# Four projections of a graph kernel: rows and weights of the next layer requested inside the layer in front of it, four count groups per row tile beside the last layer, the first prefix product moved

## The reference

```python
x1 = relu(x @ W_ah + b_ah)
for W, a_src, a_dst, b in three layers:
    h = (x1 @ W).reshape(N, 4, 192)
    as_n = (h * a_src).sum(-1)
    ad_n = (h * a_dst).sum(-1)
    # then attention over the edges
```

## Time and profile before

| | us |
|---|---|
| median of three runs | 3877.01 |
| lowest and highest | 3874.04, 3880.10 |
| the profiled execution | 3876.07 |
| its span in the profile | 3874.40 |

### The profile page before, as it was taken

The page is one execution under the profiler, slowest core; times in us unless marked ns, Lnnn a source line. Parts: engine busy times, 40 slices in busy tenths (PEclk is TensorE's granted clock), DMA queues, the critical chain, the costliest instruction groups (busy, mean ns, idle before and its releaser), DMA issues.

```text
span 3874.4 us, 59093 instructions
## 1 busy us (share of the span) xinstructions
PE 3519.8 (91%) x19026; PEld 2968.0 (77%) x19027; DVE 1948.6 (50%) x2699; ACT 1684.3 (43%) x2913; POOL 2210.9 (57%) x1621
## 2 busy tenths in 40 slices
PE   6998967999979899578888999999999999999898
PEld 3555536999979899422233599999999999999898
DVE  8244788888633545697875532332323232331034
ACT  1112687888843321277878133333333333333221
POOL 7887873666620000139991177777777777776400
PEclk9999997999999999788989999999999999999999
DMA  5343202323242311322111576767676766765421
GB/s 189 74 115 98 59 4 53 94 77 92 56 139 77 122 37 68 114 68 58 44 52 49 175 190 167 181 157 182 155 182 160 179 169 168 180 157 110 94 84 64
DMA packets 175521, 435.21 MB, mean 112 GB/s; under 512 B 39950, under 2 KB 62501, under 8 KB 175398
## 3 DMA queue, kind: packets, MB, share of 16 engines
q0 software_dynamic: 69184, 193.10, 23.3%
q1 hardware_dynamic: 91878, 214.54, 17.2%
q10 hardware_dynamic: 14336, 26.07, 1.9%
HBM read 301.01 MB, written 132.24 MB: 112 GB/s over the span
## 4 chain that ended last, share of the span: by engine, by line
PE 50%; POOL 7%; issue 3%; ACT 3%; DVE 2%; DMA 1%; SPq 0%; ACTq 0%; POOLq 0%; DVEq 0%
PE ps L2090 30%; PE ps L2077 7%; POOL xplain L1410 6%; PE ps L1684 5%; PE ps L302 4%; PE ps L310 2%; ACT work L1312 1%; ACT ps L1303 1%; POOL drec L1395 1%; PE ps L328 0%; PE ps L1249 0%; PE ps L1816 0%; DMA ct<-x_d 0%; DMA xplain<-gat_d 0%; DMA drec<-keyrow_d 0%
## 5 line engine op out<-in xcount | busy, mean ns | idle before, releaser
L2090 PE MATMUL ps<-wsplit,xsplit 128*128 x6840 | 1233.9, 337 | 0.0
L2090 PEld LDWEIGHTS ps<-wsplit,xsplit 128*128 128x128 f32 x6840 | 1179.2, 188 | 0.0
L2130 ACT ACTIVATE ct<-ps,invs 128x768 f32<-128x768 f32 x190 | 171.1, 900 | 916.5 <-PE ps L2090 916.5
L1982 DVE CAST wsplit<-wplain 128x768 fp32r<-128x768 f32 x210 | 124.6, 593 | 854.2 <-PE ps L2090 836.4
L1312 ACT ACTIVATE work<-ps,work 128x418 f32<-128x418 f32 x720 | 433.7, 620 | 158.4 <-PE ps L1220 152.7
L1259 PE MATMUL ps<-hbuf,work 128*128 128x193 f32 x2400 | 455.2, 327 | 15.6 <-DVE work L1174 13.1
L2021 POOL TENSOR_TENSOR xsplit<-ct,xsplit 128x768 fp32r<-128x768 f32 x190 | 449.0, 2363 | 0.2
L1259 PEld LDWEIGHTS ps<-hbuf,work 128*128 128x128 f32 x2400 | 407.3, 190 | 43.5 <-issue 16.9
L1160 DVE SCALAR_TENSOR_TENSOR work<-work,cnt 128x1250 f32<-128x1250 f32 x240 | 352.4, 1468 | 160.4 <-ACT work L1312 159.3
L1303 ACT ACTIVATE ps<-work,lr 128x418 f32<-128x418 f32 x720 | 426.7, 624 | 6.4 <-DMA work<-lrow_d 6.4
L2016 POOL DMA_INDIRECT ct<-x_d,relrec x190 | 205.7, 1082 | 325.7 <-PE ps L2077 321.8
(11 more groups left out here) (234 smaller groups left out, 4571.0 us busy)
## 6 DMA issues: line engine op xcount, KB each, us to landing
wplain<-in_L_gnn_W_rel SPq DMA_DIRECT2D x34, 2304.0 KB, 12.3
work<-lrow_d SPq DMA_DIRECT2D x47, 625.0 KB, 3.8
feat_d<-work ACTq DMA_DIRECT2D x30, 386.0 KB, 3.8
hbuf<-feat_d SPq DMA_DIRECT2D x60, 193.0 KB, 2.5
gat_d<-work POOLq DMA_DIRECT2D x12, 960.0 KB, 5.2
xplain<-gat_d SPq DMA_DIRECT2D x30, 384.0 KB, 3.2
work<-xa_d SPq DMA_DIRECT2D x27, 384.0 KB, 3.3
wplain<-x_d SPq DMA_DIRECT2D x20, 384.0 KB, 3.0
```

Source lines behind the costliest of these rows:

```text
L2090: last = pe.matmul(ps[:, 4 + 2 * (u % 2) + h, 0:HALF], x[:, u, c * P:(c + 1) * P], w7[:, bass.ds(base + (lo * KC * D + c * D + h * HALF), ...
```

## The change

The diff, cut where only lines move or comments differ:

```diff
+            def open_rows(self, pe):
                 pe.wait_ge(self.turned, self.b["turned"] + 0)
+                pe.sem_inc(self.turned, 2 * self.K)
+
+            def open(self, pe, rows_opened=False):
+                if not rows_opened:
+                    self.open_rows(pe)
                 pe.wait_ge(self.product, self.b["product"])
-                pe.sem_inc(self.turned, 2 * self.K)
                 pe.sem_inc(self.product, 2)
...
                     turn(0, 0, 0)
                     others_out()
                     turn(0, 1, 0)
+                    weights()
                     with pe.Fori(0, NT // 2 - 1) as i:
                         for u in range(2):
                             times(i, u)
                             turn(i + 1, u, 0)
+                    if behind is not None:
+                        behind.open_rows(pe)
                     for u in range(2):
                         times(NT // 2 - 1, u)
...
                 def times(j):
                     pe.wait_ge(self.emptied, self.b["emptied"] + j + 2)
                     for h in range(2):
+                        if h:
+                            between(j, 2)
...
                 for j in range(NT):
                     pe.wait_ge(self.taken, self.b["taken"] + j + 1)
+                    between(j, 0)
                     if j + 1 < NT:
                         turn(j + 1)
-                    between(j, 0)
+                    if j == NT - 2 and behind is not None:
+                        behind.open_rows(pe)
+                    between(j, 1)
                     times(j)
-                    between(j, 1)
+                    between(j, 3)
...
-            for u in range(2):
-                sp.wait_ge(s_x1[u], 16 * (NT // 2 + 1))
             for l in range(3):
-                if l:
-                    sp.wait_ge(W_AH.product, (W_AH if l == 1 else W_H[0]).all_products)
-                    W_H[l].load(sp)
-                sp.wait_ge(W_AH.turned, (W_AH if l == 0 else W_H[l - 1]).all_turned)
-                W_H[l].stream(sp)
+                for j in range(NT):
+                    if l == 0:
+                        sp.wait_ge(s_x1[j % 2], 16 * (j // 2 + 2))
+                    W_H[l].stream_tile(sp, j, j % 2)
+                    if l < 2 and j == 3:
+                        sp.wait_ge(W_AH.product, (W_AH if l == 0 else W_H[0]).all_products)
+                        W_H[l + 1].load(sp)
...
             W_AH.take_and_empty(act, step.loop, 2, empty_x1)
+            act.sem_inc(W_H[0].emptied, 2)
+            for u in range(2):
+                W_H[0].take(act, 0, u)
             for u in range(2):
                 act.wait_ge(s_x1[u], 16 * (NT // 2 + 1))
...
+                def counted_group(j, q):
+                    k = 4 * (j - FIRST_TILE) + q
+                    if k >= 0:
+                        act_sums(act, k, k % 2, 0)
+                        act_targets(act, step, k + 2, k % 2)
+
                 for j in range(NT):
-                    k = 2 * (j - FIRST_TILE)
-                    if j + 1 < NT:
-                        W_H[l].take(act, (j + 1) // 2, (j + 1) % 2)
-                    if k == 0:
+                    if j == FIRST_TILE:
                         act.wait_ge(s_recs, 16)
                         for q in range(2):
                             act_targets(act, step, q, q)
-                    if k >= 0:
-                        act_sums(act, k, 0, 0)
-                        act_targets(act, step, k + 2, 0)
+                    counted_group(j, 0)
+                    if j + 1 < NT:
+                        W_H[l].take(act, (j + 1) // 2, (j + 1) % 2)
+                    counted_group(j, 1)
+                    counted_group(j, 2)
                     empty_h(j, j % 2, j // 2)
-                    if k >= 0:
-                        act_sums(act, k + 1, 1, 0)
-                        act_targets(act, step, k + 3, 1)
+                    counted_group(j, 3)
...
-        BESIDE = 2 * (NT - FIRST_TILE)
+        BESIDE = 4 * (NT - FIRST_TILE)
...
-                if j == 2 and behind:
+                if (j, behind) == (0, 1):
+                    prefixes(0, R, NT)
+                if (j, behind) == (3, 3):
                     prefixes(1, 0, R)
-            prefixes(0, R, NT)
-            W_AH.multiply_single(pe, offsets)
+            W_AH.multiply_single(pe, offsets, behind=W_H[0])
             pe.wait_ge(s_offtaken, 2)
-            for s in W_H[0:2]:
-                s.multiply(pe)
+            W_H[0].multiply(pe, others_out=lambda: pe.wait_ge(W_AH.emptied, W_AH.b["emptied"] + NT + 2), rows_opened=True, behind=W_H[1])
+            W_H[1].multiply(pe, rows_opened=True, behind=W_H[2])
...
-                    pe_group(pe, 2 * (j - FIRST_TILE) + behind, behind)
-            W_H[2].multiply_single(pe, counts)
+                    pe_group(pe, 4 * (j - FIRST_TILE) + behind, behind % 2)
+            W_H[2].multiply_single(pe, counts, rows_opened=True)
...
-            for j in range(FIRST_TILE):
+            for j in range(FIRST_TILE - 1):
                 projected(2, j, j % 2)
             v.wait_ge(s_recs, 16)
             for k in range(2):
                 dve_compare(v, k, k)
+            projected(2, FIRST_TILE - 1, (FIRST_TILE - 1) % 2)
             for j in range(FIRST_TILE, NT):
-                for k in range(2 * (j - FIRST_TILE), 2 * (j - FIRST_TILE) + 2):
+                for k in range(4 * (j - FIRST_TILE), 4 * (j - FIRST_TILE) + 4):
                     dve_compare(v, k + 2, k % 2)
                     dve_add(v, step, k, k % 2)
-                    if k % 2 == 0:
-                        projected(2, j, j % 2)
+                projected(2, j, j % 2)
```

More of the change, by code:

```diff
@@ L239, in stream, with multiply, weights @@
                         self.stream_tile(sp, NT - 2 + u, u)
-            def open(self, pe):
+            def open_rows(self, pe):
                 pe.wait_ge(self.turned, self.b["turned"] + 0)
+                pe.sem_inc(self.turned, 2 * self.K)
+            def open(self, pe, rows_opened=False):
+                if not rows_opened:
+                    self.open_rows(pe)
                 pe.wait_ge(self.product, self.b["product"])
-                pe.sem_inc(self.turned, 2 * self.K)
                 pe.sem_inc(self.product, 2)
-            def multiply(self, pe, opened=False, others_out=lambda: None):
+            def multiply(self, pe, opened=False, others_out=lambda: None, rows_opened=False, behind=None):
                 K = self.K
                 if not opened:
-                    self.open(pe)
-                if self.split is None:
-                    pe.wait_ge(self.w_in, self.b[self.pick] + 16 * (K + (self.bias is not None)))
+                    self.open(pe, rows_opened)
+                def weights():
+                    if self.split is None:
+                        pe.wait_ge(self.w_in, self.b[self.pick] + 16 * (K + (self.bias is not None)))
                 def turn(i, u, r):
@@ L335, in multiply_resident, with multiply_single @@
                     self.products(pe, j, j % 2)
[L337 to L344, removed]
+            def multiply_single(self, pe, between, rows_opened=False, behind=None):
+                self.open(pe, rows_opened)
                 def turn(j):
@@ L564, in act_phase1 @@
             for l in range(3):
-                act.sem_inc(W_H[l].emptied, 2)
+                if l:
+                    act.sem_inc(W_H[l].emptied, 2)
                 def empty_h(j, u, i):
@@ L579, in act_phase1 @@
                 if l < 2:
-                    W_H[l].take_and_empty(act, step.loop, 4, empty_h)
+                    W_H[l].take_and_empty(act, step.loop, 4, empty_h, taken=0 if l else 2)
                     continue
```

## The result

| | before | after |
|---|---|---|
| median, us | 3878.56 (3874.04 to 3883.88, 4 runs) | 3844.18 (3840.93 to 3846.95, 4 runs) |
| profiled execution / its span | 3876.07 / 3874.4 | 3841.89 / 3840.3 |
| first product starts | 32.93 | 24.63 |
| next stage starts | 589.73 | 556.27 |
| from there to the end of the span | 3284.7 | 3284.0 |

The ratio is 0.9909, 95% [0.9896, 0.9921]: 34 us faster. The forecast of 3843 is 1.2 off. The profiled execution lost 34.2 us, 33.5 of them in the edited stage. The same measure is used for every experiment: "stage end" is the start of the first instruction of the next stage, since the remaining 3280 us differ by several microseconds between the profiled executions of the kernels here (3277.1 to 3290.5).

A forecast was written before the change was run, and what follows sets the result against it. PE was taken to bound the first 590 us. Start 8.0, boundaries 16.4 and groups 9.0 sum to 33.4 off 3876.07, giving 3842.7, plus 0.9 against the median: 3843 us, range 3834 to 3862.

The forecast's parts named there:

- The start: Before the first product: rows opened ahead of any prefix, first product at 24.9 instead of 32.93; 8.0 us saved after corrections.
- The slower first product: At the start: PE idles ahead of the prefix and may run more at the low clock; 1.0 us lost.
- the wait for row tile 4: In the first product stage: PE's wait of 0.95 us at 67.05 should go.
- The boundaries: Three gaps between products: rows requested two products ahead, leaving gaps of 2.75, 2.6 and 3.3 us; 16.4 saved.
- open_rows: PE waits three times for its own last transposes; between nothing and 0.82 us each, 0.2 each taken.
- The groups: Beside layer 2 and behind it: four groups a round instead of two, rounds of 19.76 us; 9.0 saved.
- the first group: Group 0 behind tile 1's product: a wait of 3.8 us for ACT, then 3.5 us long.
- 16 groups moved save 57.6, the longer rounds take back 48: Beside layer 2: 16 groups at 3.6 us moved into the rounds, against eight rounds each 6.0 longer.
- The longer round: Rival, beside layer 2: third group's compare comes late, 2.1 us in each of eight rounds, 17 back, 3860; chance 0.13.
- The clock swings: Rival, in the rounds: frequent small idles put PE at the low clock; at a third of the work 3888; chance 0.04.
- POOL's records: Rival: relation records arrive after 577.50 whatever PE does and later stages wait, up to 25 us lost, 3868; chance 0.04.
- The three bounds: Uncertainties of the start's clock, open_rows and group 0, giving some 7 us either way; own range 3835 to 3851.

The follow-up runs named there:

- Experiment 1: Changed kernel with the start undone: destinations' prefix back ahead of the rows, relations' prefix behind tile 2; 3852.33 us, ratio 0.9936 to the kernel before.
- Experiment 3: Changed kernel with early rows undone and open() again raising turned only behind both waits; 3865.66 us, ratio 0.9963 to the kernel before.
- experiment 2: Changed kernel with early rows undone by order only, open() keeping its new order of raise and wait; 3849.92 us, ratio 0.9932 to the kernel before.
- experiment 4: Kernel before, with only the raise of turned moved ahead of the wait for product in open() and multiply_single(); 3865.38 us, ratio 0.9961.
- Experiment 5: Changed kernel with two groups a tile and DVE's old order; 3851.9 us, ratio 0.9937 to the kernel before.
- experiment 9: Four groups a tile with layer 2's product in thirds, as in experiment 7, but begun at tile 1; 3826.63 us, ratio 0.9857 to the kernel before.
- experiment 10: Five groups a tile with the product in quarters, as in experiment 8, but begun at tile 1; 3824.39 us, ratio 0.9854 to the kernel before.
- Experiment 12: Changed kernel with fifty extra memsets on POOL ahead of its scatter of the relation records; single run, 3845.93 us.
- experiment 6: Changed kernel with three groups a tile in place of four; 3840.25 us, ratio 0.9902 to the kernel before.
- experiment 7: Changed kernel with layer 2's product cut into thirds, so no two of the four groups are back to back; 3833.44 us, ratio 0.9882 to the kernel before.
- experiment 8: Changed kernel with five groups a tile and layer 2's product cut into quarters; 3823.54 us, ratio 0.9851 to the kernel before.

## Why the prediction was right, point by point

- **The start: 8.0 forecast.** The end of the first weight's last product moved from 142.71 to 134.28: 8.4. Rows were not the limit, the prefix at 23.76 was. The product came at 24.63, 8.3 earlier (8.0 counted). The slower first product took 6.01 - 5.12 = 0.9 of it (1.0 counted), and the wait for row tile 4 (0.95) went. That this is the low clock is not shown: the granted clock of both profiles reads 1.00 up to there, although the first turns (1.54) take nearly twice the 0.82 of later ones in both kernels. The relations' prefix came 3.5 later (68.97 for 65.46) where some 2 were counted, and nothing waited for it. Experiment 1: 8.1.
- **The boundaries: 16.4 forecast.** Gaps of 2.44, 2.55 and 3.27 against 2.75, 2.6 and 3.3 counted. Savings: 9.05 + 9.37 - 2.44 - 8.00 = 8.0; 6.49 + 8.30 - 2.55 - 8.00 = 4.2, 0.3 more than counted, since the product behind that gap was slow before too; 7.44 + 9.04 - 3.27 - 7.91 = 5.3. open_rows cost 0.5 at each of two layers (0.2 at each of three counted): the row of 204.46 starts 1.12 behind its last turn, where other products start 0.65 behind theirs, and the two products in it take 15.72 in place of 15.65. That leaves 16.5. Experiment 3: 16.9, of which 16.0 are the boundaries'. **The reason was half wrong.** The prediction put all of it down to requesting the rows two products ahead. For the second and third boundary the raise inside open() was enough, with no request ahead of it (experiments 2 and 4). Only the first needs the rows requested tile by tile as x1 is stored; this is argued from SP's wait for the stores, and no run takes that part alone.
- **The groups: 9.0 forecast.** From the end of tile 1's product to the last group: 24.4 for the first round, 138.6 for seven, 11.8 to group 34, 49.6 for the 14 behind it; together 224.4. Before it was 232.8 (the prediction's 233.0 starts at a turn that overlaps the end of the product, 0.17 early), so 8.4 are saved, and 0.2 more between the last group and the next stage. Counted were 23.3, 138.3, 12.0 and 50.4. The mis-sized term is the first group: 4.23 idle and 4.16 long where 3.8 and 3.5 stood. Experiment 5: 9.0.
- **"16 groups moved save 57.6, the longer rounds take back 48"** holds and hides that the two groups are not alike: the third per tile saves about 3.55 for 16.00 - 13.76 = 2.24, the fourth 3.55 to 3.7 for 3.81.
- **The longer round** did not come. The compare of the third group is in time: DVE ends it some 1.6 us before PE wants it at 401.67, as counted.
- **The clock swings** did not come in the rounds: 1.00 over 138.7 us with idles of 1.40 and 0.70 in every one. The Trainium skill, TensorE: Matmul & The Clock Gate, "A second HAM failure mode: psum-queue depth-cycling", did not apply here. Where the clock did fall, it was not in the rounds: in the changed kernel at the first group, behind 4.23 us of idle (0.86 from 326.4 to 350.6), and at the group behind the attention sums, behind 3.52 (0.50 from 497 to 499); in experiments 5, 9 and 10 at the third boundary, where PE has only two turns to do in some 3.3 us (0.50, 0.51 and 0.50 from 311 to 313).
- **POOL's records.** "After 577.50 whatever PE does" was wrong, if harmless. In 305 to 500 us POOL issued 111 scatters where it had issued 119, beside a DVE with more to do per microsecond, and behind 567 eight of them took 2.64 each. Experiment 12 says that this costs nothing that can be measured.
- **The range was wider than its working.** The three bounds that it names sum to 2.2 us down and 3.9 up (0.5, 0.6, 1.1 and 1.0, 1.9, 1.0), where "some 7 either way" was written. That all three sums came within half a microsecond is luck in part: the first group cost 1.1 more than counted, and the groups behind the rounds took back 0.8.

## What to carry to other kernels

Ask, at each semaphore that PE raises, which wait stands in front of it in PE's own stream: a request that needs nothing of the running matmuls should be raised ahead of the wait for them. Work filled into a longer operation pays only if every copy of its single PSUM place finds a piece of that operation beside it; count what the round grows by against what the tail loses, group by group, since the fourth, back to back with another (3.81 for about 3.6), gained nothing clear over three, and five in four cuts won. Compare such variants by the end of the edited stage, and subtract what its rows show to be the clock's.

## What was not expected of the hardware

- **PE's stream runs ahead of its queued matmuls.** A raise that stands behind a product was taken about 6 us before that product's last matmul ended: rows requested at 221.07 against an end at 226.9, and 228.27 against 234.1. A raise is no sign that the work in front of it is done.
- **A scatter takes longer to issue beside some of DVE's work.** POOL's timeline of the changed kernel, as DVE turns from the counts to the masks of the attention:

```profile
560.51 1.19 POOL L820 DMA_INDIRECT relrec_d<-work  x1 [0.30 <-issue]
...
567.87 2.64 POOL L820 DMA_INDIRECT relrec_d<-work  x1 [0.30 <-issue]
570.82 2.64 POOL L820 DMA_INDIRECT relrec_d<-work  x1 [0.30 <-issue]
...
593.91 1.19 POOL L820 DMA_INDIRECT relrec_d<-work  x1 [0.30 <-issue]
...
598.95 0.60 POOL L808 DMA_DIRECT2D relrec<-relrec_d  x1 [2.01 <-DMA relrec_d<-work]
```

The same instruction takes 1.19 and 2.64 us. DVE there repeats a compare of 0.83 and a custom operation of 1.46 us every 2.95 us (compares at 566.39 and 569.34), and the scatters start every 2.95 us as well. The Trainium skill, SBUF — State Buffer, "Who interferes with whom", says that a transfer issued from GpSimd is held up while DVE holds the port pair that the two share. The equal periods fit that; no run here separates it from other causes.
- **A gap of the same length leaves the clock up or not.** Behind the third boundary the same product took 7.91 in the changed kernel and in experiments 6, 7 and 8, and 9.26, 9.02 and 9.25 in experiments 5, 9 and 10, which issue the same work on PE up to there. With the turn in front that is 1.7 us of luck in a stage end, and the first group adds as much again (2.40 or 4.16).
